# Mixed pieces added to x + bias in DRAM by accumulating transfers, first products of half sums copied by ScalarE

## The reference, cut to what matters

```
agg_w = einsum('bk,koi->boi', att, weight)      # att from a small MLP on cond
c     = einsum('boi,bih->boh', agg_w, x) + agg_b[:, :, None]
x     = x + (c @ W.T + bias + sum_e w_e * (c @ A_e.T) @ Bf_e.T)
z     = grouped conv over x (9 taps, 4 groups) + context + bias
x     = x + unperm(gelu(perm(z) @ up) @ down)
```

## Time and profile before

| what | value |
|---|---|
| median of 3 runs | 2671.96 us (2670.89 to 2673.55) |
| profiled execution | 2673.87 us |
| its span in the trace | 2672.1 us |
| mean granted clock of TensorE | 0.986 of full speed |
| TensorE matmuls busy | 2562.1 us (96%) |
| VectorE busy | 2118.2 us (79%) |
| ScalarE busy | 1160.4 us (43%) |
| GpSimd busy | 1130.3 us (42%) |
| DMA queues of SP, ACT, POOL | 47.0%, 16.1%, 8.1% of 16 engines' span |

### The profile page before, as it was taken

How to read it: one execution, slowest core, us unless ns; L and a number is a source line. 1 busy time by engine, 2 the same in 40 slices (tenths; PEclk the granted TensorE clock), 3 DMA queues, 4 the chain that set the end, 5 groups by cost and what they waited for, 6 DMA issues and landing times. The chain is left out here.

```text
span 2672.1 us, 39300 instructions
## 1 busy us (share of the span) xinstructions
PE 2562.1 (96%) x11458; PEld 2070.7 (77%) x11458; DVE 2118.2 (79%) x2975; ACT 1160.4 (43%) x1905; POOL 1130.3 (42%) x879
## 2 busy tenths in 40 slices
PE   7899999999999999999999889999999999999997
PEld 6678887888867778778888668888888888888775
DVE  6778778777787778897878657888888888888776
ACT  3222223222243344543444555555555555555563
POOL 4546631664238685555656532222222222222231
PEclk9999999999999999999999899999999999999998
DMA  8887778887786676767575664476767676777686
GB/s 286 291 278 256 261 224 281 274 272 248 231 285 206 219 237 195 264 193 222 180 214 181 195 196 132 143 222 204 225 206 220 208 222 205 226 217 220 187 275 240
DMA packets 456155, 603.98 MB, mean 226 GB/s; under 512 B 40328, under 2 KB 265920, under 8 KB 455936
## 3 DMA queue, kind: packets, MB, share of 16 engines
q1 hardware_dynamic: 347984, 379.24, 47.0%
q10 hardware_dynamic: 86544, 154.26, 16.1%
q0 software_dynamic: 21408, 67.88, 8.1%
HBM read 372.63 MB, written 228.59 MB: 225 GB/s over the span
## 5 line engine op out<-in xcount | busy, mean ns | idle before, releaser
L478 PE MATMUL ps_c<-w_hi,ring_hi 128*128 128x512 f32 x1792 | 710.4, 396 | 11.7 <-DVE ring_lo L960 9.7
L478 PE MATMUL ps_c<-w_hi,ring_lo 128*128 128x512 f32 x1792 | 708.8, 396 | 0.0
L478 PE MATMUL ps_c<-w_lo,ring_hi 128*128 128x512 f32 x1792 | 707.8, 395 | 0.0
L611 ACT ACTIVATE ring_hi<-raw_n 128x512 fp32r<-128x512 f32 x384 | 242.8, 634 | 740.2 <-PE ps_c L478 457.1
L1407 POOL DMA_INDIRECT y_d<-y_s,idx x128 | 147.1, 1149 | 741.0 <-ACT y_s L1578 665.0
L960 DVE TENSOR_TENSOR ring_lo<-raw_n,ring_hi 128x512 fp32r<-128x512 f32 x384 | 363.2, 946 | 88.2 <-ACT ring_hi L611 83.4
L1545 ACT ACTIVATE kern<-ps_up 128x512 f32<-128x512 f32 x512 | 306.2, 598 | 263.9 <-PE ps_up L1425 251.0
L478 PEld LDWEIGHTS ps_c<-w_hi,ring_hi 128*128 128x128 f32 x1792 | 337.8, 188 | 98.3 <-DVE ring_lo L960 18.4
L478 PEld LDWEIGHTS ps_c<-w_lo,ring_hi 128*128 128x128 f32 x1792 | 337.8, 189 | 79.3 <-issue 0.5
L478 PEld LDWEIGHTS ps_c<-w_hi,ring_lo 128*128 128x128 f32 x1792 | 337.7, 188 | 79.2
L1653 DVE TENSOR_TENSOR g_lo<-kern,g_hi 128x512 fp32r<-128x512 f32 x512 | 354.5, 692 | 40.0 <-ACT g_hi L1549 23.7
(11 more groups left out here) (225 smaller groups left out, 4577.2 us busy)
## 6 DMA issues: line engine op xcount, KB each, us to landing
raw_n<-in_x_t SPq DMA_DIRECT2D x128, 512.0 KB, 5.8
u_s<-x_d SPq DMA_DIRECT2D x496, 64.0 KB, 2.1
z_d<-x_s SPq DMA_DIRECT2D x120, 256.0 KB, 3.9
rear<-y_d SPq DMA_DIRECT2D x112, 256.0 KB, 3.1
rear<-x_d SPq DMA_DIRECT2D x112, 256.0 KB
out_dram<-results SPq DMA_DIRECT2D x112, 256.0 KB
u_s<-in_x SPq DMA_DIRECT2D x64, 256.0 KB, 5.6
x_d<-r_early ACTq DMA_DIRECT2D x64, 256.0 KB, 4.1
```

The source lines that it names most:

```text
L478: mm = nc.tensor.matmul(bank, a[:, dc, :], w[k][:, dc, :], start=(first and dc == 0 and n == 0), stop=(dc == 3 and n == 2), skip_group_che ...
L611: nc.scalar.activation(ring_hi[g % RING][:].rearrange("p a n -> p (a n)"), ring_raw[p][k], ACT.Copy).then_inc(hi_ready, 1)
```

## The change

`xb_d` goes, and a scratch `half_d` comes: the half sums go there, and x + bias is stored in `x1_d` itself in quads 0 to 15. In quads 16 to 31 nothing is loaded into `res` and nothing is added to it on GpSimd. Instead `take_mixed` writes agg_b * rs + the mixed piece into `res` in one operation (scalar_tensor_tensor; one operand from SBUF, one from PSUM, agg_b as a scalar per partition), and GpSimd issues a DMA that adds `res` to the piece in `x1_d` (`store_mixed`, accum_op add). `add_bias_of_mix` on ScalarE goes. The second copy of rs has a room of its own (`mix`). Besides, the copies of first products in quads 0 to 15 (`take` for k = 0, 2, 3, 5) move from VectorE to ScalarE.

```diff
@@ -199,7 +200,8 @@
         sums = [kern[:, HALF:L], kern[:, 0:HALF]]
-        bias_s = rs_s = x_n2[:, 0, :]
+        bias_s = x_n2[:, 0, :]
+        rs_s = [bias_s, mix[:].rearrange("p m n -> p (m n)")]
         res = [sh.u_s[:, 1028:1540], sh.u_s[:, 1540:2052], x_n2[:, 1, 0:512], x_n2[:, 1, 512:1024]]
         raw = [raw_n1[:, 0, :], raw_n2[:, 0, :], raw_n1[:, 1, :], raw_n2[:, 1, :]]
...
@@ -262,7 +265,7 @@
             n = 8 * q + PIECES.index((blk, p))
             b, half = batch(q, 2 * p + blk // 2), HALVES[sweep(q)][0]
-            return x1_d[b, :, 2 * half + blk % 2, :]
+            return half_d[b, :, 2 * half + blk % 2, :]
         def v_room_free(eng, q, p, blk):
...
@@ -350,8 +353,8 @@
                     if m >= 2:
                         sp.wait_ge(aggw_mm, 8)
-                wait(sp, sh.res_out[m], 16 * (n // 4))
-                sp.dma_start(res[m], piece(x.rearrange("b c (s q) -> b c s q", s=S) if n < 8 * FINAL else xb_d, n)).then_inc(res_in[m], 16)
+                wait(sp, xb_out[m], 16 * (n // 4))
+                sp.dma_start(res[m], piece(x.rearrange("b c (s q) -> b c s q", s=S), n)).then_inc(res_in[m], 16)
             def load_r(q, p, blk):
...
@@ -415,16 +418,13 @@
                 for n in biased_at(q, t, 0):
                     load_res(n)
-                for n in range(8 * FINAL, 8 * QUADS):
-                    if mix_slot(n - 4) + 5 == ITEMS * q + t:
-                        load_res(n)
                 for n in range(EARLY if q == QUADS - 1 else 0):
                     if t == ((5, 5, 5, 6, 7)[n] if n < 5 else 7 + (n - 4) // 2):
...
                     if t == 10:
                         for m in range(4):
-                            sp.wait_ge(sh.res_out[m], 16 * 2 * 25)
+                            sp.wait_ge(sh.res_out[m], 16 * 2 * (25 - FINAL))
                         sp.wait_ge(sh.pad_ready, 3)
                     sh.load_group(sp, x1_d, sh.xp[t - 10], t - 10, 0, t - 10)
...
@@ -662,37 +662,28 @@
                 nc.scalar.activation(v_hi[n % 2][:], r_s[p][blk], ACT.Copy).then_inc(vhi_ready, 1)
-            def e_room(n):
-                if n < 8 * 24:
-                    return sums[0][:, n % 2 * 512:(n % 2 + 1) * 512]
-                return aggw_stage[n % 2]
             def take_rows(half):
                 act.wait_ge(rs_mm, half + 1)
...
                     act.wait_ge(res_set, 8 * FINAL)
                 else:
-                    act.wait_ge(e_ready, 64)
-                nc.scalar.activation(rs_s, ps_v[:, 0, :], ACT.Copy).then_inc(rs_ready, 1)
-            def add_bias_of_mix(n):
-                b, half, sub = place_of(n)
-                act.wait_ge(rs_ready, half + 1)
-                act.wait_ge(res_set, n - 1)
-                if n == 8 * FINAL:
-                    act.wait_ge(mlp_act, 4)
-                if n == 8 * 24:
                     act.wait_ge(mix_out, 16 * 24)
-                nc.scalar.activation(e_room(n), rs_s[:, sub * 512:(sub + 1) * 512], ACT.Identity,
-                                     scale=aggb_s[:, b:b + 1]).then_inc(e_ready, 1)
-            def store_res(n):
-                if n < 8 * FINAL:
-                    act.wait_ge(res_set, n + 1)
-                else:
-                    act.wait_ge(mixed, n - 8 * FINAL + 1)
-                act.dma_start(piece(xb_d if n < 8 * FINAL else x1_d, n), res[n % 4]).then_inc(sh.res_out[n % 4], 16)
+                nc.scalar.activation(rs_s[half], ps_v[:, 0, :], ACT.Copy).then_inc(rs_ready, 1)
+            def store_biased(n):
+                act.wait_ge(res_set, n + 1)
+                act.dma_start(piece(x1_d, n), res[n % 4]).then_inc(xb_out[n % 4], 16)
+            def take(q, t):
+                k, p = t // 2, t % 2
+                blk = {0: R11, 2: R12, 3: R22, 5: R21}[k]
+                act.wait_ge(item_mm, ITEMS * q + t + 1)
+                v_room_free(act, q, p, blk)
+                if q == 0 and blk in (R12, R21):
+                    room_free(act, blk - R12)
+                read = y_read if k == 3 else u_read
+                nc.scalar.activation(r_s[p][blk], ps_y[p] if k == 3 else ps_u[p], ACT.Copy).then_inc(read[p], 1)
             def load_tw(n, k):
...
@@ -722,12 +713,13 @@
                 if ahead and ahead != (0, 0):
                     split(*ahead)
+                done = product_from(q, t, -1)
+                if done and done[0] < FINAL and done[1] // 2 in (0, 2, 3, 5):
+                    take(*done)
                 for n in mixed_at(*divmod(ITEMS * q + t + 1, ITEMS)):
                     split_v(n)
                 if q in (FINAL, FINAL + 8) and t == 6:
                     take_rows(q // 8 - 2)
-                for n in mixed_at(q, t):
-                    add_bias_of_mix(n)
                 if FINAL <= q < QUADS and t == 5:
                     split_agg(q)
...
@@ -743,11 +735,8 @@
                 if 0 <= q - 1 < FINAL and t in (0, 1):
                     store_r(q - 1, t, R12)
-                for n in range(8 * FINAL, 8 * QUADS):
-                    if mix_slot(n) + 3 == ITEMS * q + t:
-                        store_res(n)
                 for n in biased_at(q, t, 4):
-                    store_res(n)
+                    store_biased(n)
                 if q == 0 and t in (3, 4, 6, 7):
                     for n in range(2):
...
@@ -817,11 +806,14 @@
                 nc.gpsimd.tensor_tensor(a12, a12, s2, ALU.subtract).then_inc(s_ready, 1)
-            def add_e(n):
-                e = sums[0][:, n % 2 * 512:(n % 2 + 1) * 512] if n < 8 * 24 else aggw_stage[n % 2]
-                pool.wait_ge(res_in[n % 4], 16 * (n // 4 + 1))
-                pool.wait_ge(e_ready, n - 8 * FINAL + 1)
-                nc.gpsimd.tensor_tensor(res[n % 4], res[n % 4], e, ALU.add).then_inc(res_set, 1)
+            def store_mixed(n):
+                i = n - 8 * FINAL
+                pool.wait_ge(mixed, i + 1)
+                if i == 0:
+                    for m in range(4):
+                        pool.wait_ge(xb_out[m], 16 * 2 * FINAL)
+                pool.dma_start(piece(x1_d, n), res[n % 4], accum_op=ALU.add).then_inc(sh.res_out[n % 4], 16)
             def mix_piece(q, c):
...
@@ -884,8 +875,9 @@
                 if mixes(q) and t in (2, 9):
                     mix_piece(q, t // 9)
-                for n in mixed_at(*divmod(ITEMS * q + t - 1, ITEMS)):
-                    add_e(n)
+                for n in range(8 * FINAL, 8 * QUADS):
+                    if mix_slot(n) + 3 == ITEMS * q + t:
+                        store_mixed(n)
                 if 24 <= q < 29 and t == 7:
                     prepare_layer1(q - 24)
...
@@ -999,12 +991,6 @@
                 dve.wait_ge(item_mm, ITEMS * q + t + 1)
                 if k in (0, 2, 3, 5):
-                    if q < FINAL:
-                        v_room_free(dve, q, p, blk)
-                        if q == 0 and blk in (R12, R21):
-                            room_free(dve, blk - R12)
-                        nc.vector.tensor_copy(r_s[p][blk], bank).then_inc(read, 1)
-                        return
                     dve.wait_ge(r_in[p][blk], 16 * (q - FINAL + 1))
                 elif k in (1, 6):
...
@@ -1025,10 +1011,20 @@
             def take_mixed(n):
                 i = n - 8 * FINAL
+                b, half, sub = place_of(n)
                 dve.wait_ge(mix_mm, i + 1)
-                dve.wait_ge(res_set, n + 1)
-                nc.vector.tensor_tensor(res[n % 4], ps_w[n % 4], res[n % 4], ALU.add).then_inc(mixed, 1)
+                if i == 0:
+                    dve.wait_ge(mlp_act, 4)
+                if i < 4:
+                    dve.wait_ge(xb_out[i], 16 * 2 * FINAL)
+                else:
+                    dve.wait_ge(sh.res_out[n % 4], 16 * (i // 4))
+                if i % 64 == 0:
+                    dve.wait_ge(rs_ready, i // 64 + 1)
+                nc.vector.scalar_tensor_tensor(res[n % 4], rs_s[i // 64][:, sub * 512:(sub + 1) * 512], aggb_s[:, b:b + 1],
+                                               ps_w[n % 4], ALU.mult, ALU.add).then_inc(mixed, 1)
             def split_tw(n, k, part):
...
@@ -1043,7 +1039,7 @@
             def slot(q, t):
                 done = product_from(q, t, -1)
-                if done:
+                if done and (done[0] >= FINAL or done[1] // 2 in (1, 4, 6)):
                     take(*done)
                 ahead = product_from(q, t, 3)
```

More of the change, by code:

```diff
@@ L145, in layer0_block @@
 def layer0_block(nc, sh, x, x_t, cond_w, bias_k, cond_t, w0, b0, w1, b1, w2, b2, w_t, bias, lora_a, lora_b, coeffs, scales,
-                 conv_w, ctx_w, fside, ident, up, down, aggw_d, weff_d, t_d, xb_d, x1_d):
+                 conv_w, ctx_w, fside, ident, up, down, aggw_d, weff_d, t_d, half_d, x1_d):
     with ExitStack() as ctx:
@@ L228, in layer0_block @@
         bias_in, sums_ready, rs_mm, rs_ready = sem("bias_in"), sem("sums_ready"), sem("rs_mm"), sem("rs_ready")
-        res_in, res_set, e_ready, mixed = [sem(f"res_in{m}") for m in range(4)], sem("res_set"), sem("e_ready"), sem("mixed")
```

(13 more changed lines are left out.)

## The result

The changed kernel takes 2678.8 us in the median of seven runs (2673.6 to 2682.4), the kernel before 2668.0 (2665.0 to 2673.6, seven runs as well). The ratio is 1.0036, with a 95% interval of 1.0022 to 1.0051: slower by about 10 us, where I had forecast 31 us faster. The profiled executions (2673.9 before, 2675.5 after) lie closer together than the medians: that of before lies above all seven of its timed runs, and its layer 1, which has the same program in both, is 5 us longer in its trace (1152.3 us from its first matmul to the end, against 1147.1). So the places are read in layer 0.

A forecast was written before the change was run, and what follows sets the result against it. TensorE was taken as the bound, with 60.8 us at most to regain in five stretches of layer 0. 5 + 1 + 14 + 5.5 + 6 = 31.5 us off 2673.9 gave 2642.4, stated as 2641 against the median; range 2624 to 2667.

The forecast's parts named there:

- A: Layer 0, 425 to 475 us, first change of sweeps: TensorE loses 8.6 us, of which 5 should come back.
- B: Layer 0, 750 to 785 us, second change of sweeps: TensorE loses 8.6 us, of which 1 should come back.
- D: Layer 0, 1125 to 1165 us, third change of sweeps: TensorE loses 11.8 us, of which 5.5 should come back.
- the copies on ScalarE: Quads 0 to 15: 128 copies leave VectorE, giving 5 us at the first change of sweeps, 1 at the second.
- C: Layer 0, 820 to 1000 us, quads that mix pieces and prepare weights: TensorE loses 16.2 us; 14 should come back.
- The issue on GpSimd: Accumulating issue in GpSimd's list: taken as 1.0 us, between 0.5 and the replaced addition's 1.6, so GpSimd gains either way.
- The adding transfer: Quads 16 to 31: each store likeliest 2 units of 0.9 us of all DMA engines, landing 2.7 to 9.7 us; no cost.
- The share stays 0.66: DMA engines' share in a quad of the last sweep: unchanged if an accumulating transfer takes 2 units.
- rival 2: Wait moves instead of going: VectorE still stands at `take_mixed`, now for the accumulating store's landing; 2661 us, chance 0.13.
- rival 1: Accumulating transfer is dear: from k = 4.1 quads 16 to 31 run at the DMA engines' pace; 2764 us, chance 0.12.
- E: Layer 0, 1500 to 1520 us, last mixes and passage to layer 1: TensorE loses 15.6 us; 6 should come back.
- Slower: Whole kernel slower by more than 0.2% (5 us), through a dear accumulating transfer or slow new VectorE operation; chance 0.14.

The follow-up runs named there:

- Run 1: Changed kernel, but the 128 stores of mixed pieces are plain ones from ScalarE's queue, none from GpSimd, none adding: 2628.6 us, ratio 0.9838.
- Run 5: Kernel before, plus 32 small plain GpSimd transfers (16 KB each) in the first four quads of the second half: 2683.5 us, ratio 1.0055.
- run 3: Changed kernel, plus a one-column write and a wait for it behind each of GpSimd's first 120 issues: 2649.4 us, ratio 0.9919.
- run 8: Changed kernel with plain instead of adding stores from GpSimd, and the one-column write and wait behind each of its first 120 issues: 2635.0 us, ratio 0.9874.
- run 4: Changed kernel, but the last four stores of layer 0 are plain ones from ScalarE's queue: 2676.2 us, ratio 1.0026.
- run 2: Changed kernel, but GpSimd issues its 128 stores as plain ones, without adding: 2649.3 us, ratio 0.9921.
- run 6: Kernel before, plus 32 small plain GpSimd transfers, each followed by a one-column write and a wait for it: 2679.3 us, ratio 1.0032.
- run 9: Changed kernel, plus the pause behind GpSimd's issues, and the last six mixed pieces stored from ScalarE's queue without GpSimd: 2638.8 us, ratio 0.9895.
- run 10: Changed kernel with the last six mixed pieces stored without GpSimd, and no pause: 2671.9 us, ratio 1.0016.

## Why the prediction was wrong

- **A, B, D and the copies on ScalarE: right.** 5.3 + 0.9 + 5.5 us against 5 + 1 + 5.5, and the copies alone 5.7 against 6 (4.0 of it in A, 0.4 in B).
- **C, 14 of 16.2: the mechanism right, the outcome wrong.** Run 1 shows that without load, e and addition all of 16.2 goes. In the change C loses 12.5 us more than before (800 to 1010 us).
- **"The issue on GpSimd ... I take 1.0: GpSimd gains either way": the step that failed.** Its length was about right (0.88 to 0.90 us), its effect wasn't. I priced it by the time that it takes in GpSimd's list, and read from the earlier trace rows that VectorE beside an issue stays at 0.68. Behind those four issues come three one-column writes and a single addition (1172.49 us), so there was no run to be shut out for. What counts is what follows in the list: with sums right behind an issue, VectorE's next operation with two SBUF inputs lasts until GpSimd stops. Run 5 makes it in the kernel before, run 3 takes it from the change: 29 of the 50 us between the change and run 1, of which 15 fall away as well where only the adding goes.
- **The sum as it should have been.** The relief was worth 41 us (run 1), not 31. Against it stand three terms that the sum has at nothing: 43 for the shut-outs and the adding (14 each alone, 15 more for the two together), 6 to 7 for leaving the layer behind GpSimd's stores. 41 less 50 leaves a change that is slower by some 10 us.
- **The rule from *SBUF — State Buffer*, "Who interferes with whom" (the Trainium skill), was half of it.** That the two engines shut each other out for a whole instruction agrees with each chain without an issue (1.2 to 1.8 us), and that one SBUF input is untouched with scalar_tensor_tensor's 737 ns. Behind an issue the measurement goes further: over four sums and two issues, 7.2 us. By the rule one could see who would be hit and not how hard.
- **The adding transfer.** I took k = 2 units of 0.9 us of all engines. The unit was rough: 44.4 us at the 202 GB/s of the earlier trace rows are 9.0 MB and not 8.4, and in the kernel before SP's loads take 0.90 us of all engines for each 256 KB but ScalarE's stores 0.69 (48.76 MB at 52.3% and 14.99 MB at 12.4% of 320 us). Measured: 320 us x 0.361 for 15.62 MB is 1.94 us for each 256 KB, k = 2.2; plain from the same queue 0.71 us (run 8). "The share stays 0.66" was wrong in its small part (0.73), and "I take no cost" in its large one: x lands later, and the adding is worth 14 us between runs 3 and 8. The landing (4.9 to 5.6 us in the median) was far under the 12.7 us allowed, and `take_mixed` waited for it once, 2.2 us: rival 2 did not happen, nor did rival 1. *Collectives: The Full Stack* in the Trainium skill, section "The bandwidth ceiling: the fold count and why AG ≠ RS ≠ AR" (two source reads for an add), gave k of 1.5 to 2 as an estimate; the trace has 2.2 in all, and 2.7 times the plain one.
- **E, 6 of 15.6: half right, and a wait was missed.** The stalls shrank by 3 us, but I had not asked what leaving layer 0 waits for. With GpSimd's transfers still under way the block's end comes 8.0 us behind its last issue, where before it came 1.9 us behind VectorE's last operation and 2.70 behind GpSimd's. Three runs order it: 14.35 us of wait with landings of about 5 us, 10.26 with plain ones, 3.46 with none under way. But the landing is not the whole of it: the end comes 8.0, 7.4 and 7.2 us behind the last adding issue (change, runs 3 and 4) and 6.5 behind the last plain one (runs 2 and 8), and runs 5 and 6 have 5.31 us behind GpSimd's last operation with nothing under way. What these 5.31 us are is open; in runs 9 and 10 they are hidden, since there GpSimd's last operation ends 8.2 and 6.4 us before the block does.
- **The slower side.** "Slower" had 0.14, for a dear transfer or a slow scalar_tensor_tensor (737 ns, no cost). That VectorE could be slower because GpSimd issues more had no case at all. (The chances were also added loosely: 0.80 for faster holds 0.05 of rival 2's 0.13 and not most of it.)

## What to carry to other kernels

Price a GpSimd DMA issue by what stands behind it in GpSimd's list: if that is a run of operations on SBUF, put a stop between them (a one-column write and a wait for its semaphore were enough), or expect a VectorE operation with two SBUF inputs that starts behind the issue to last until GpSimd next stops. In a list that others already wait for, the pause may cost what it saves (run 6). Let the last transfer that GpSimd issues, and GpSimd's last operation, lie well before a block ends. And when a change puts another kind of instruction in the place of one that it takes away, price what it does to the neighbours and not only its length: here additions of 1.6 us became issues of 0.9 us and GpSimd's longest unbroken run in C fell from 22 to 7.5 us, yet VectorE's longest operation went from 1.8 to 7.2 us.

## What the runs showed that I had not expected

- In these traces GpSimd shuts VectorE out for more than one operation only behind an issue: runs of 22 us without one let it in after each operation (up to 1.82 us), runs of 3 to 7 us with one don't (2.8 to 7.2 us). 32 plain issues of 16 KB cost a kernel 14 us.
- A longer list cures it: 120 writes of 0.41 us and their waits make the kernel 29 us faster (14 with plain stores).
- An adding store holds the DMA engines 2.7 times as long as a plain one from the same queue (1.94 against 0.71 us of all engines for each 256 KB), and takes 0.88 us to issue instead of 0.56.
- A block's end comes 8.0 us behind the last adding issue of GpSimd and 6.5 us behind the last plain one, while with plain stores from ScalarE's queue it comes 0.8 us (run 9) or 1.9 us (before) behind VectorE's last operation. Even 32 issues that had long landed put GpSimd's own share of it from 2.70 to 5.31 us (runs 5 and 6).
